# Scan stage: expanding an operand one chunk later on GpSimd, and loading it ahead of the values on SyncE

## The chip, the core and the metric

The kernel runs on one core of a Trainium2 chip. A core has TensorE (matmuls; PE in the profile, PEld for its weight loads), VectorE (DVE), ScalarE (ACT), GpSimd (POOL) and SyncE (SP), which issues the transfers between the device memory and the on-chip memory here. Each engine runs its own list of instructions in order; they wait for each other by semaphores. The metric is the device time of one execution in microseconds (us), as a median of several runs.

## The reference

A transformer block with adaptive layer norms: a linear-attention layer with a recurrent state, then two local-attention and feed-forward layers. Only the recurrence matters for this change. For each of 2 batches and 16 heads, with a state `s` of 16 x 16 and 4096 time steps:

```
def step(s, inp):
    q_, w_, k_, v_, a_, b_ = inp
    sa = einsum('bhij,bhj->bhi', s, a_)
    s = s * w_[:, :, None, :] + sa[..., None] * b_[:, :, None, :] + v_[..., None] * k_[:, :, None, :]
    return (s, einsum('bhij,bhj->bhi', s, q_))
```

The inputs of the step (q, w, k, v, a, b) are made by projections of a mixed `x` in the stage before; the output y goes through a group norm and a gate in the stage behind.

## The kernel before

The kernel has stages one after the other: setup, mix (the projections), scan (the recurrence), gate, and local (the two layers). The change is in the scan stage alone (`scan_stage`, lines 876 to 1489).

**Chunks and units.** The 4096 steps are cut into 256 chunks of 16 steps. Four chunks are a unit (`UC` = 4), and there are 64 units (`NU`), named by a pair: window `w` and half `k` (0 or 1). `shift(w, k, units)` names a unit further on. The state is carried from chunk to chunk, so the chunks of all heads run one after the other; within a chunk the work is matrix products of 32 x 32 blocks.

**The work of one chunk n.** TensorE (`chunk`, lines 1190 to 1219) runs ten groups of 32 small matmuls each. In order, by the tile they write: `P` from the state and `ax` (the second half of P; its first half, from `vc` and `d_ak`, was done at the end of the chunk before), `Y` from the state and `qx`, `Y` from `vc` and `d_qk`, `SA`, `S` from `vc` and `kT`; then `products` (lines 1160 to 1171) for a chunk 16 ahead, n + 16 (`LEAD` = 4 units ahead), which writes `AB` from `aq` and the expanded operands `bx` and `kx`; then `S` from `sa` and `bT`, and `Y` from `sa` and `d_qb`, whose end is signalled as `y_ps`; last the first half of P of chunk n + 1. The product AB of a chunk has to be known so early because it is masked, sent through device memory, inverted on VectorE (`solve`) and read back before the chunk itself runs. `products(n + 16)` stands in the loop only for the first 240 chunks.

**GpSimd** runs two kinds of work. `use(n)` expands the operands `ax`, `qx`, `bT` and `kT` of chunk n (six instructions) into buffers that exist twice, so it first waits for `y_ps` of chunk n - 2 (line 1124). `prepare(m)` expands `bx` and `kx` of chunk m (two instructions) from the tile `early` and signals `bk_x`, for which `products(m)` on TensorE waits (line 1162); it first waits for the transfer of `early` (line 1114) and for the product of chunk m - 2. ScalarE copies the third operand of the product, `aq`, from the same tile (`copy_aq`), at the end of each chunk, 17 chunks ahead.

**ScalarE** also copies the small results out of the matmul banks (`p`, `sa`, `y`) and the values `v` of the next chunk into `vc` (`copy_v`), for which the first half of P waits. **VectorE** keeps the state, masks AB, expands `d_ak` and `d_t`, and solves.

**SyncE** issues all transfers of the stage in one hand-written order (`unit`, lines 1060 to 1085). In each unit (w, k) it loads what the next unit needs (`part`, `tt`, `gl`), a problem for `solve`, on odd units (k = 1) four stores of y here and on even ones at the end, then in two halves (j = 0 and 1, two chunks each) `load_v` for the next unit, `load_early` for the unit five ahead and, after the first half, `load_late` (`late` and `tok`, for the unit two ahead), and at the end it stores a solution and the masked product (`pose`). `load_early(j)` waits until the product that reads the tile now is done (line 964); `load_v(j)` until ScalarE has copied the values that the tile holds now.

Of the kernel before, what the change touches and what calls it, by code (L numbers as in the profile page):

```python
# [875 lines left out]
def scan_stage(nc, persist, a, T):  # L876

    NU = 2 * (T // P)
    UC = NCH // 2
    BG = NB * CC  # L880
    LEAD = 4
    const, ident = persist["const"], persist["ident"]
    with ExitStack() as ctx:
# [44 lines left out]
        def shift(w, k, units):  # L928
            return w + (k + units) // 2, (k + units) % 2

        def first_chunk(w, k):
            return w * NCH + k * UC

        def bg(t):
            return t.rearrange("p b g i -> p (b g) i")
# [12 lines left out]
        def exists(w, k, units):  # L948
            return not isinstance(w, int) or 2 * w + k + units < NU

        with nc.Block() as block:
            @block.sync
            def _(sp):
# [8 lines left out]
                def load_early(w, k, j):  # L962

                    sp.wait_ge(S["ab_ps"].sem, S["ab_ps"].after(first_chunk(w, k) + 2 * j + 1, UC))
                    sp.sem_inc(s_free, 1)
                    sp.dma_start(early[j][:].rearrange("p c x b g y t -> p (c x b g y t)"),
                                 a["cm"][bass.ds(w, 1), :, k * UC + 2 * j:k * UC + 2 * j + 2].rearrange("o p c x b g y t -> (o p) (c x b g y t)")
                                 ).then_inc(pair["early_in"][j].sem, 16)
# [18 lines left out]
                def load_gl(w, k):  # L987
                    freed("s_sb", first_chunk(w, k) - 1 - UC)
                    sp.dma_start(gl[k][:].rearrange("p c q -> p (c q)"),
                                 a["gl"][bass.ds(w, 1), :, k * UC:(k + 1) * UC].rearrange("o p c b g -> (o p) (c b g)")  # L990
                                 ).then_inc(Hf["gl_in"][k].sem, 16)

                def load_part(w, k):

                    sp.wait_ge(Hf["part_out"][k].sem, Hf["part_out"][k].after(w))
                    for name in ("d_ak", "d_qk", "d_qb"):
                        freed(name, first_chunk(w, k) - 1 - UC)
                    sp.dma_start(part[k][:].rearrange("p c q z t -> p (c q z t)"),
                                 a["part"][bass.ds(w * 2 + k, 1)].rearrange("o p n -> (o p) n")).then_inc(Hf["part_in"][k].sem, 16)
# [10 lines left out]
                def load_problem(w, k):  # L1010
                    sp.wait_ge(Hf["att_out"][k].sem, Hf["att_out"][k].after(w))
                    sp.wait_ge(Hf["solved"][k].sem, Hf["solved"][k].after(w, 1))
                    sp.dma_start(prob[k][:, 0:SQ], a["att"][bass.ds(w * 2 + k, 1)].rearrange("o q h m t -> (o q h) (m t)")
                                 ).then_inc(Hf["prob_in"][k].sem, 16)

                def store_solution(w, k):
                    sp.wait_ge(Hf["solved"][k].sem, Hf["solved"][k].after(w))
                    sp.dma_start(a["inv"][bass.ds(w * 2 + k, 1)].rearrange("o q h m t -> (o q h) (m t)"), sol[k][:, 0:SQ]
                                 ).then_inc(Hf["inv_out"][k].sem, 16)

                def load_t(w, k):
                    sp.wait_ge(Hf["inv_out"][k].sem, Hf["inv_out"][k].after(w))
                    freed("d_t", first_chunk(w, k) - 1 - UC)
                    sp.dma_start(tt[k][:], a["inv"][bass.ds(w * 2 + k, 1)].rearrange("o (c q) h m t -> (o h m) c q t", c=UC)
                                 ).then_inc(Hf["tt_in"][k].sem, 16)

                def store_y(w, heads):
                    sp.wait_ge(Hf["yn"][1].sem, Hf["yn"][1].after(w))
                    for h in heads:
                        sp.dma_start(a["y_tok"][bass.ds(w, 1), :, :, :, :, h].rearrange("o t c b g i -> (o t) (c b g) i"),  # L1030
                                     yn[h * CH:(h + 1) * CH].rearrange("t c q i -> t (c q) i")).then_inc(y_out.sem, 16)
# [28 lines left out]
                def unit(w, k):  # L1060
                    heads = (range(HP // 2, HP) if k else range(HP // 2)) if not isinstance(w, int) or w > 0 else range(0)
                    if exists(w, k, 1):
                        n1 = shift(w, k, 1)
                        load_part(*n1)
                        load_t(*n1)
                        load_gl(*n1)
                    if exists(w, k, 3):
                        load_problem(*shift(w, k, 3))
                    if k and len(heads):
                        store_y(w - 1, heads)  # L1070
                    for j in range(UC // 2):
                        if exists(w, k, 1):
                            load_v(*shift(w, k, 1), j)
                        if exists(w, k, LEAD + 1):
                            load_early(*shift(w, k, LEAD + 1), j)
                        if j == 0 and exists(w, k, 2):
                            load_late(*shift(w, k, 2))
                    if exists(w, k, 2):
                        store_solution(*shift(w, k, 2))
                    if exists(w, k, LEAD):  # L1080
                        pose(*shift(w, k, LEAD))
                    if not k and len(heads):
                        store_y(w - 1, heads)
                    if not exists(w, k, LEAD):
                        fetch_weights(NU - 2 * w - k - 1)
# [19 lines left out]
            @block.gpsimd  # L1105
            def _(pool):
                def expand(dst, src):
                    return nc.gpsimd.tensor_tensor(dst[:], src.unsqueeze(2).broadcast_to([P, BG, HQ, CH]),  # L1108
                                                   headmask[:].unsqueeze(1).unsqueeze(3).broadcast_to([P, BG, HQ, CH]), ALU.mult)

                def prepare(w, k, c):

                    m = first_chunk(w, k) + c
                    pool.wait_ge(pair["early_in"][c // 2].sem, pair["early_in"][c // 2].after(w * 2 + k))
                    pool.wait_ge(S["ab_ps"].sem, S["ab_ps"].after(m, 2))
                    expand(bx[c % 2], bg(early[c // 2][:, c % 2, 1, :, :, 0, :]))
                    expand(kx[c % 2], bg(early[c // 2][:, c % 2, 1, :, :, 1, :])).then_inc(S["bk_x"].sem, 1)

                def use(w, k, c):

                    n = first_chunk(w, k) + c
                    if c == 0:
                        pool.wait_ge(Hf["late_in"][k].sem, Hf["late_in"][k].after(w))
                    pool.wait_ge(S["y_ps"].sem, S["y_ps"].after(n, 2))
                    expand(ax[c % 2], bg(late[k][:, c, :, :, 0, :]))
                    expand(qx[c % 2], bg(late[k][:, c, :, :, 1, :])).then_inc(S["ax_x"].sem, 1)
                    for dst, x in ((bT, 0), (kT, 1)):
                        for b in range(NB):
                            last = nc.gpsimd.tensor_tensor(  # L1129
                                dst[c % 2][:, b * CC:(b + 1) * CC], tok[k][:, c, b, x].unsqueeze(2).broadcast_to([P, CC, HQ, HS]),  # L1130
                                headmask[:].unsqueeze(1).unsqueeze(3).broadcast_to([P, CC, HQ, HS]), ALU.mult)
                    last.then_inc(S["kT_x"].sem, 1)

                pool.wait_ge(s_c, 48)
                for u in range(LEAD):
                    for c in range(UC):
                        prepare(u // 2, u % 2, c)
                prepare(LEAD // 2, 0, 0)
                use(0, 0, 0)
                use(0, 0, 1)  # L1140

                def unit(w, k):
                    for c in range(UC):
                        if c < UC - 1 and exists(w, k, LEAD):
                            prepare(*shift(w, k, LEAD), c + 1)
                        if c == UC - 1 and exists(w, k, LEAD + 1):
                            prepare(*shift(w, k, LEAD + 1), 0)
                        if c + 2 < UC:
                            use(w, k, c + 2)
                        elif exists(w, k, 1):  # L1150
                            use(*shift(w, k, 1), c + 2 - UC)

                halfwise(pool, unit)

            @block.tensor
# [1557 lines left out]
```

## Time and profile before

| | before |
|---|---|
| time, median of 3 runs | 5328.73 us (5325.01 to 5329.86) |
| profiled execution, its own time | 5325.01 us |
| its span (first to last instruction) | 5323.2 us |
| TensorE busy | 4869.5 us, 91% |
| VectorE busy | 3583.0 us, 67% |
| ScalarE busy | 3186.1 us, 60% |
| GpSimd busy | 2317.0 us, 44% |
| mean granted TensorE clock | 0.952 of full |

The profile also cuts the span into 40 slices of 133 us. The scan stage runs from slice 8 to slice 17 (about 960 to 2145 us): there TensorE is at 8 or 9 tenths, VectorE at 7, ScalarE at 4 or 5, GpSimd at 6 or 7, and the 16 DMA engines move 142 to 166 GB/s at a busy share of 6 or 7 tenths. So in this stage no engine is full, and the waits of each engine for the others have to be read. The local stage behind it (from about 2370 us) is most of the span, with TensorE over 9 tenths.

A busy share of TensorE counts overlapping matmuls once; its ends are modelled. "Idle before, releaser" in a row says how long the engine stood before the instruction and what ended that; "issue" means that the profile shows nothing that it waited for.

### The profile page before, as it was taken

The page shows a single profiled execution, that of the slowest core. Times are in us where ns is not written, and L with a number is a line of the kernel's source. Part 1 is how long each engine was busy: PE and PEld are TensorE (multiplying, and loading weights), DVE is VectorE, ACT ScalarE, POOL GpSimd, SP SyncE. Part 2 cuts the span into 40 slices and gives each one's busy share as a digit, 9 for nine tenths or more (in the row PEclk, how much of TensorE's full clock was granted, in tenths as well). Part 3 has the DMA queues.
Part 4 walks back from the last instruction along what each step waited for, and adds up shares of the span by engine and source line. Part 5 has one row for each costly group of instructions (what it writes and reads, how often), then busy time and mean ns, then how long its engine had stood idle before and what let it go on. Part 6 is the DMA issues. An engine that isn't in the chain of part 4 may idle for free. (4 is left out here: it accounts for less than half of the span.)

```text
span 5323.2 us, 277799 instructions
## 1 busy us (share of the span) xinstructions
PE 4869.5 (91%) x111000; PEld 4118.3 (77%) x111000; DVE 3583.0 (67%) x11241; ACT 3186.1 (60%) x8874; POOL 2317.0 (44%) x3833
## 2 busy tenths in 40 slices
PE   7988888588888888659999999999999999999999
PEld 6888888578888887547777777777777777777777
DVE  5666666577777776556666666666666666666665
ACT  5777777344444444346666666666666666666665
POOL 1222222466666666004444444444444444444443
PEclk8999999699999998779999999999999999999999
DMA  2433343677777777760000000000100000000000
GB/s 81 99 90 93 94 99 86 142 165 156 166 163 166 157 166 161 221 203 14 15 15 12 15 15 15 15 15 16 46 23 21 21 21 17 21 21 21 19 20 18
DMA packets 993729, 389.81 MB, mean 73 GB/s; under 512 B 773840, under 2 KB 938448, under 8 KB 992464
## 3 DMA queue, kind: packets, MB, share of 16 engines
q1 hardware_dynamic: 992256, 385.96, 30.7%
q14 instruction: 188, 1.54, 0.1%
q10 hardware_dynamic: 1232, 1.45, 0.1%
q8 instruction: 53, 0.87, 0.1%
HBM read 217.51 MB, written 169.74 MB: 73 GB/s over the span
## 5 line engine op out<-in xcount | busy, mean ns | idle before, releaser
L2303 ACT ACTIVATE l_prob<-l_prob,l_nb,l_rq 128x256 f32<-128x256 f32 x1024 | 604.6, 592 | 279.8 <-DVE l_nb L2089 278.2
L1954 POOL TENSOR_TENSOR l_pn<-l_prob,l_rinv 128x512 f32<-128x512 f32 x512 | 532.5, 1040 | 331.0 <-DVE l_rinv L2069 327.4
L2499 PE MATMUL lD<-l_hid,w 128*128 128x128 f32 x3072 | 384.8, 275 | 0.0
L2499 PEld LDWEIGHTS lD<-l_hid,w 128*128 128x128 f32 x3072 | 363.1, 192 | 0.2 <-issue 0.2
L2287 ACT COPY l_qT<-lA 128x512 f32<-128x512 f32 x128 | 74.9, 585 | 389.5 <-PE lA L2407 389.5
L1961 POOL TENSOR_TENSOR l_x1s<-l_x 128x128 f32<-128x128 f32 x128 | 58.0, 453 | 493.5 <-DVE l_x L2127 493.2
L497 POOL TENSOR_TENSOR rk<-rk,bkraw 128x256 f32<-128x256 f32 x64 | 54.6, 872 | 477.7 <-DVE bkraw L383 477.7
L2491 PE MATMUL lA<-l_hn,w 128*128 128x128 f32 x2048 | 258.2, 279 | 2.0 <-POOL l_hn L1972 2.0
L2465 PE MATMUL lB<-l_oT,wo 128*128 128x128 f32 x2048 | 259.9, 275 | 0.0
L2398 PE MATMUL lA<-wqkv,l_h 128*128 128x512 f32 x512 | 243.6, 598 | 16.4 <-DVE l_mask L2170 16.4
L2491 PE MATMUL lB<-l_hn,w 128*128 128x128 f32 x2048 | 249.6, 275 | 0.0
L2491 PEld LDWEIGHTS lA<-l_hn,w 128*128 128x128 f32 x2048 | 239.8, 192 | 9.4 <-POOL l_hn L1972 2.5
L2465 PEld LDWEIGHTS lB<-l_oT,wo 128*128 128x128 f32 x2048 | 243.7, 192 | 0.0
L1979 POOL TENSOR_TENSOR l_outt<-l_t,l_xat 128x256 f32<-128x256 f32 x64 | 46.4, 724 | 452.7 <-DVE l_t L2163 452.7
L2398 PE MATMUL lB<-wqkv,l_h 128*128 128x512 f32 x512 | 242.2, 595 | 0.0
L2398 PE MATMUL lC<-wqkv,l_h 128*128 128x512 f32 x512 | 240.6, 592 | 0.0
L2491 PEld LDWEIGHTS lB<-l_hn,w 128*128 128x128 f32 x2048 | 238.8, 192 | 0.0
L1451 DVE TENSOR_TENSOR sc_ssum<-sc_S,sc_state 128x64 f32<-128x64 f32 x256 | 57.0, 223 | 243.6 <-PE sc_S L1177 243.2
L1129 POOL TENSOR_TENSOR sc_kT<-sc_tok,sc_headmask 128x64 f32<-128x64 f32 x512 | 217.1, 443 | 0.0
L1108 POOL TENSOR_TENSOR sc_ax<-sc_late,sc_headmask 128x128 f32<-128x128 f32 x256 | 104.1, 407 | 236.2 <-PE sc_Y L1177 233.6
L2491 PE MATMUL lC<-l_hn,w 128*128 128x128 f32 x1536 | 205.3, 283 | 0.0
L1966 POOL TENSOR_TENSOR l_dsqs<-l_dsq 128x128 f32<-128x128 f32 x128 | 58.8, 459 | 333.2 <-ACT l_dsq L2316 333.2
(298 smaller groups left out, 15753.2 us busy)
## 6 DMA issues: line engine op xcount, KB each, us to landing
scratch_cm<-cm SPq DMA_DIRECT2D x64, 512.0 KB, 4.5
sc_early<-scratch_cm SPq DMA_DIRECT2D x128, 256.0 KB, 3.8
scratch_part<-sc_att SPq DMA_DIRECT2D x64, 512.0 KB, 6.4
sc_part<-scratch_part SPq DMA_DIRECT2D x64, 512.0 KB, 5.0
scratch_tok<-vt SPq DMA_DIRECT2D x512, 48.0 KB, 1.8
l_h<-scratch_h SPq DMA_DIRECT2D x128, 129.0 KB, 2.6
scratch_gr<-gr SPq DMA_DIRECT2D x64, 256.0 KB, 2.0
sc_late<-scratch_cm SPq DMA_DIRECT2D x64, 256.0 KB, 4.3
```

The lines of the kernel that those rows point to most:

```text
L1108: return nc.gpsimd.tensor_tensor(dst[:], src.unsqueeze(2).broadcast_to([P, BG, HQ, CH]), headmask[:].unsqueeze(1).unsqueeze(3).broadcast_t ...
L1129: last = nc.gpsimd.tensor_tensor(dst[c % 2][:, b * CC:(b + 1) * CC], tok[k][:, c, b, x].unsqueeze(2).broadcast_to([P, CC, HQ, HS]), headma ...
L1451: nc.vector.tensor_tensor(s_sum[:], first16(S_ps), state[c % 2][:], ALU.add).then_inc(S["s_sum"].sem, 1)
L1954: tt(pn[s][:, pair], prob[s][:, pair], rinv[s][:, pair].unsqueeze(2).broadcast_to([P, 2, 2 * P]), ALU.mult).then_inc(Q["pn"][s].sem, 1)
L1961: tt(x1s[s][:], shifted(x1[s][w])[:, 0:P], shifted(x1[s][w])[:, P:2 * P], ALU.add).then_inc(S["x1_sum"][s].sem, 1)
L1966: tt(dsqs[s][:], dsq[s][:, 0], dsq[s][:, 1], ALU.add).then_inc(S["dsq_sum"][s].sem, 1)
L2287: nc.scalar.copy(qT[s][:].rearrange("p h t -> p (h t)"), bank[s][0][:]).then_inc(S["qT"][s].sem, 1)
L2303: last_ = nc.scalar.activation(prob[s][:, h], prob[s][:, h], ACT.Exp, scale=rq8[s][:, h:h + 1], bias=nb[s][:, h:h + 1], accum_out=sums[s][ ...
L2398: last_ = mm(bank[s][j][:], h[:, k * P:(k + 1) * P], wqkv[:, k, j * INNER:(j + 1) * INNER], start=(k == 0), stop=(k == CC - 1))
L2465: last_ = mm(bank[s][1][:, m * P:(m + 1) * P], wo[:, k, m * P:(m + 1) * P], oT[s][:, k], start=(k == 0), stop=(k == NHP - 1))
L2491: last_ = mm(bank[s][j][0:MW, at:at + P], w1[:, k, tile * MW:(tile + 1) * MW], hn[s][:, k], start=(k == 0), stop=(k == CC - 1))
L2499: last_ = mm(bank[s][3][:, c * P:(c + 1) * P], w2[:, m, c * P:(c + 1) * P], hid[s][:, m], start=(c == 0 and m == 0), stop=(c == CC - 1 and ...
```

## The change

Two edits, both in `scan_stage`. On SyncE, `load_early` moves ahead of `load_v` in each half of a unit. On GpSimd, the preamble no longer prepares a 17th chunk, and in the loop the iteration of chunk n calls `prepare(n + 16)` and then `use(n + 2)`, where it called `prepare(n + 17)` and then `use(n + 2)`. ScalarE's `copy_aq` stays 17 chunks ahead, and TensorE's order is not touched.

```diff
--- before.py
+++ after.py
@@ -1069,10 +1069,10 @@
                     if k and len(heads):
                         store_y(w - 1, heads)
                     for j in range(UC // 2):
+                        if exists(w, k, LEAD + 1):
+                            load_early(*shift(w, k, LEAD + 1), j)
                         if exists(w, k, 1):
                             load_v(*shift(w, k, 1), j)
-                        if exists(w, k, LEAD + 1):
-                            load_early(*shift(w, k, LEAD + 1), j)
                         if j == 0 and exists(w, k, 2):
                             load_late(*shift(w, k, 2))
                     if exists(w, k, 2):
@@ -1135,16 +1135,13 @@
                 for u in range(LEAD):
                     for c in range(UC):
                         prepare(u // 2, u % 2, c)
-                prepare(LEAD // 2, 0, 0)
                 use(0, 0, 0)
                 use(0, 0, 1)
 
                 def unit(w, k):
                     for c in range(UC):
-                        if c < UC - 1 and exists(w, k, LEAD):
-                            prepare(*shift(w, k, LEAD), c + 1)
-                        if c == UC - 1 and exists(w, k, LEAD + 1):
-                            prepare(*shift(w, k, LEAD + 1), 0)
+                        if exists(w, k, LEAD):
+                            prepare(*shift(w, k, LEAD), c)
                         if c + 2 < UC:
                             use(w, k, c + 2)
                         elif exists(w, k, 1):
```

GpSimd's list, from the place where the preamble has issued `use(0)`. The digit behind a name is the buffer: chunk parity for `ax`, `bx` and so on, the half of a unit for `early`. Before:

```order
L1108 TENSOR_TENSOR sc_ax1<-sc_late0,sc_headmask 128x128 [waits sc_y_ps0]
L1108 TENSOR_TENSOR sc_qx1<-sc_late0,sc_headmask 128x128
L1129 TENSOR_TENSOR sc_bT1<-sc_tok0,sc_headmask 128x64 x2
L1129 TENSOR_TENSOR sc_kT1<-sc_tok0,sc_headmask 128x64 x2
L1108 TENSOR_TENSOR sc_bx1<-sc_early0,sc_headmask 128x128 [waits sc_ab_ps0,sl_early_in0]
L1108 TENSOR_TENSOR sc_kx1<-sc_early0,sc_headmask 128x128
L1108 TENSOR_TENSOR sc_ax0<-sc_late0,sc_headmask 128x128 [waits sc_y_ps0]
L1108 TENSOR_TENSOR sc_qx0<-sc_late0,sc_headmask 128x128
L1129 TENSOR_TENSOR sc_bT0<-sc_tok0,sc_headmask 128x64 x2
L1129 TENSOR_TENSOR sc_kT0<-sc_tok0,sc_headmask 128x64 x2
L1108 TENSOR_TENSOR sc_bx0<-sc_early1,sc_headmask 128x128 [waits sc_ab_ps0,sl_early_in1]
L1108 TENSOR_TENSOR sc_kx0<-sc_early1,sc_headmask 128x128
```

and now, from the same `use(1)`:

```order
L1108 TENSOR_TENSOR sc_ax1<-sc_late0,sc_headmask 128x128 [waits sc_y_ps0]
L1108 TENSOR_TENSOR sc_qx1<-sc_late0,sc_headmask 128x128
L1129 TENSOR_TENSOR sc_bT1<-sc_tok0,sc_headmask 128x64 x2
L1129 TENSOR_TENSOR sc_kT1<-sc_tok0,sc_headmask 128x64 x2
L1108 TENSOR_TENSOR sc_bx0<-sc_early0,sc_headmask 128x128 [waits sc_ab_ps0,sl_early_in0]
L1108 TENSOR_TENSOR sc_kx0<-sc_early0,sc_headmask 128x128
L1108 TENSOR_TENSOR sc_ax0<-sc_late0,sc_headmask 128x128 [waits sc_y_ps0]
L1108 TENSOR_TENSOR sc_qx0<-sc_late0,sc_headmask 128x128
L1129 TENSOR_TENSOR sc_bT0<-sc_tok0,sc_headmask 128x64 x2
L1129 TENSOR_TENSOR sc_kT0<-sc_tok0,sc_headmask 128x64 x2
L1108 TENSOR_TENSOR sc_bx1<-sc_early0,sc_headmask 128x128 [waits sc_ab_ps0,sl_early_in0]
L1108 TENSOR_TENSOR sc_kx1<-sc_early0,sc_headmask 128x128
```

Between `use(1)` (buffers 1) and `use(2)` (buffers 0) stood the expansion for chunk 17 (`bx1`), with that of chunk 16 done ahead of `use(0)`; now the expansion for chunk 16 (`bx0`) stands there. From here on every `bx`, `kx` pair belongs to the chunk one lower than before.

SyncE's list in the middle of a unit, the loads for the values, the early and the late operands, to the store of a solution. Before:

```order
L973 DMA sc_v0<-scratch_tok 128x4x32 [waits sc_v_c0]
L966 DMA sc_early0<-scratch_cm 128x512 [waits sc_ab_ps0]
L980 DMA sc_late0<-scratch_cm 128x4x128 [waits sc_kT_x0]
L983 DMA sc_tok0<-scratch_tok 128x8x64
L973 DMA sc_v1<-scratch_tok 128x4x32 [waits sc_v_c0]
L966 DMA sc_early1<-scratch_cm 128x512 [waits sc_ab_ps0]
L1018 DMA scratch_inv<-sc_sol0 128x256 [waits mxb_k30]
```

and now:

```order
L966 DMA sc_early0<-scratch_cm 128x512 [waits sc_ab_ps0]
L973 DMA sc_v0<-scratch_tok 128x4x32 [waits sc_v_c0]
L980 DMA sc_late0<-scratch_cm 128x4x128 [waits sc_kT_x0]
L983 DMA sc_tok0<-scratch_tok 128x8x64
L966 DMA sc_early1<-scratch_cm 128x512 [waits sc_ab_ps0]
L973 DMA sc_v1<-scratch_tok 128x4x32 [waits sc_v_c0]
L1018 DMA scratch_inv<-sc_sol0 128x256 [waits mxb_k30]
```

`early0` and `v0` have changed places, and so have `early1` and `v1`; `v1` now stands behind the wait for the product that `early1` waits for, and in front of the stores.

## Rows read from the trace of the kernel before

**Rows 1.** Busy time by stretch: columns stretch, length, engines, clock, DMA share, GB/s

```profile
1020.00:2060.00 1040.00, 897.01 (x75225) 834.25 (x75227) 806.70 (x2401) 503.80 (x2285) 723.17 (x1878) 0.93 0.77 162
1510.00:1516.00 6.00, 5.39 (x361) 5.19 (x365) 1.74 (x8) 2.14 (x10) 3.95 (x13) 0.50 1.10 217
```

**Rows 2.** Waits, 1020 to 2060: who waited for whom, total us, times, longest

```profile
POOL sc_ax L1108 <- PE sc_Y L1177: 193.2, 172, 8.0
POOL sc_bx L1108 <- DMA sc_early<-scratch_cm: 124.3, 37, 5.2
ACT sc_vc L1265 <- DMA sc_v<-scratch_tok: 61.9, 28, 3.1
ACT sc_aq L1259 <- DMA sc_early<-scratch_cm: 44.9, 29, 2.6
PE sc_P L1177 <- ACT sc_vc L1265: 19.9, 19, 1.9
PE sc_SA L1177 <- ACT sc_p L1282: 18.5, 24, 1.8
```

**Rows 3.** GpSimd's instructions in a chunk, timeline: start us, us, engine, line

```profile
1558.45 0.40 POOL L1108 TENSOR_TENSOR sc_ax<-sc_late,sc_headmask 128x128 f32<-128x128 f32 x1 [1.02 <-PE sc_Y L1177]
...
1559.90 1.38 POOL L1129 TENSOR_TENSOR sc_kT<-sc_tok,sc_headmask 128x64 f32<-128x64 f32 x2
1561.25 0.40 POOL L1108 TENSOR_TENSOR sc_bx<-sc_early,sc_headmask 128x128 f32<-128x128 f32 x1
1561.61 0.40 POOL L1108 TENSOR_TENSOR sc_kx<-sc_early,sc_headmask 128x128 f32<-128x128 f32 x1
```

**Rows 4.** TensorE, the same chunk

```profile
1557.86 0.48 PE L1177 MATMUL sc_Y<-sc_sa,sc_d_qb 32*32 32x32 f32 x32
1560.60 0.42 PE L1169 MATMUL sc_AB<-sc_aq,sc_bx 32*32 32x32 f32 x29 [0.15 <-issue]
1561.47 0.48 PE L1177 MATMUL sc_Y<-sc_sa,sc_d_qb 32*32 32x32 f32 x32
```

**Rows 5.** GpSimd and TensorE in the preamble: a wait on the expanded operand

```profile
986.01 0.43 POOL L1108 TENSOR_TENSOR sc_kx<-sc_early,sc_headmask 128x128 f32<-128x128 f32 x1
986.69 0.55 PE L1169 MATMUL sc_AB<-sc_aq,sc_bx 32*32 32x32 f32 x25 [2.67 <-POOL sc_kx L1108]
```

**Rows 6.** The chunk that waits for transfers, timeline, SyncE, ScalarE, GpSimd, TensorE

```profile
1509.25 0.45 PE L1177 MATMUL sc_P<-sc_vc,sc_d_ak 32*32 32x32 f32 x32 [1.07 <-ACT sc_vc L1265]
...
1542.12 0.40 SPq L973 DMA_DIRECT2D sc_v<-scratch_tok  x1
1542.88 0.33 SPq L966 DMA_DIRECT2D sc_early<-scratch_cm  x1
1544.51 0.24 ACT L1265 COPY sc_vc<-sc_v 128x64 f32<-128x64 f32 x1 [2.42 <-DMA sc_v<-scratch_tok]
1546.53 0.30 ACT L1259 COPY sc_aq<-sc_early 128x128 f32<-128x128 f32 x1 [1.20 <-DMA sc_early<-scratch_cm]
1546.59 0.40 POOL L1108 TENSOR_TENSOR sc_bx<-sc_early,sc_headmask 128x128 f32<-128x128 f32 x1 [3.90 <-DMA sc_early<-scratch_cm]
1547.30 0.40 POOL L1108 TENSOR_TENSOR sc_ax<-sc_late,sc_headmask 128x128 f32<-128x128 f32 x1
1549.38 0.40 POOL L1108 TENSOR_TENSOR sc_kx<-sc_early,sc_headmask 128x128 f32<-128x128 f32 x1
1544.90 0.45 PE L1177 MATMUL sc_P<-sc_vc,sc_d_ak 32*32 32x32 f32 x32 [1.30 <-ACT sc_vc L1265]
1548.29 0.65 PE L1169 MATMUL sc_AB<-sc_aq,sc_bx 32*32 32x32 f32 x32
1549.56 0.66 PE L1177 MATMUL sc_Y<-sc_sa,sc_d_qb 32*32 32x32 f32 x32
```

**Rows 7.** SyncE's queue, the unit before the next such place

```profile
1559.13 0.37 SPq L973 DMA_DIRECT2D sc_v<-scratch_tok  x1
1561.59 0.35 SPq L966 DMA_DIRECT2D sc_early<-scratch_cm  x1
```

## The prediction

> **What bounds the kernel now.** I read the waits of the scan stage first, then the busy time of one long stretch, then the timeline of single chunks on GpSimd, TensorE and SyncE.
>
> The stretch from 1020 to 2060 us holds 235 chunks (GpSimd's 1878 instructions there over 8 per chunk), so a chunk takes 1040.0 / 235 = 4.43 us [rows 1]. No engine is full in it: TensorE 897 us, VectorE 807, GpSimd 723. In the waits the reader sees two things [rows 2]. GpSimd stands idle before `ax` 172 times, 193.2 us, for the `Y` matmuls of TensorE: once per chunk it goes through its list, and then waits for the next `y_ps`. And there are waits for transfers: GpSimd before `bx` for `early` (37 times, 124.3 us), ScalarE for `v` (28 times, 61.9 us) and for `early` (29 times, 44.9 us). About 29 times is once in two units, that is once in eight chunks. Little of it reaches TensorE: 19.9 us behind the copied `v`, 18.5 us behind `p`.
>
> What that one chunk costs shows in rows 6: `v` is issued at 1542.12, copied at 1544.51 after 2.42 us of waiting, and TensorE starts at 1544.90, 1.30 us late. The stretch from the last end of `Y` to this one (1543.6 to 1550.2) is 6.6 us long. In the same place of the period before, 35 us earlier, TensorE waits 1.07 us for `vc` until 1509.25 [rows 6]; from 1510 the granted clock is 0.50 for 6 us, the level of 1.2 GHz, while TensorE is busy 5.39 of them [rows 1]. Such a chunk costs some 2.2 us more than the mean one. GpSimd's 3.9 us of waiting for `early` are not on the path: its `ax` (1547.30) is for a later chunk.
>
> The order around `products` decides the rest. In a chunk without stalls `Y` ends at 1557.86 + 0.48 = 1558.34, the matmuls of AB start at 1560.60, and the next `Y` ends at 1561.95 [rows 4]: 2.26 us, then 1.35 us. GpSimd starts `ax` at 1558.45, 0.11 us behind the first `Y`, and ends `kx` at 1562.01 [rows 3], 1.41 us after AB has started. That is harmless today, because this `kx` belongs to the chunk after.
>
> **The change on GpSimd.** The instructions are the same but for one pair in the preamble; the numbers of the pairs move. `use(n + 1)` waits for `y_ps(n - 1)` and now `prepare(n + 16)` stands behind it, where `prepare(n + 17)` stood. TensorE needs `bk_x(n + 16)` in the middle of chunk n. So a ring closes within one chunk: the end of `Y` of n - 1, six instructions of `use`, two of `prepare`, AB, `S`, `Y` of n. Before, a whole chunk lay between `kx` and its matmuls. The ring in four terms:
> - end of `Y` to `ax`: 0.11 us [rows 3, 4].
> - GpSimd's eight instructions: 723.17 us over 235 chunks, 3.08 us [rows 1]. Bounds: the shortest pass, the one behind the stall, is 1547.30 to 1549.78, 2.48 us [rows 6]; the pass in rows 3, with a pair of `kT` at 1.38 us, is 3.56. I take the mean, since the trigger (`y_ps`) and the list are unchanged and VectorE's work behind the same `y_ps` is too.
> - end of `kx` to AB: `kx` ends at 986.44 and AB starts at 986.69, 0.25 us [rows 5].
> - AB to the end of `Y`: 1.35 us [rows 4]; at the low clock 1548.29 to 1550.22, 1.93 us [rows 6]. The mean granted clock of 0.93 [rows 1] means the low level in 14% of the time, so 0.14 x 0.58 = 0.08 more.
>
> The ring is 0.11 + 3.08 + 0.25 + 1.35 + 0.08 = 4.87 us, against 4.43 for a mean chunk now, stalls included: +0.44. TensorE will stand before AB in nearly every chunk. With the two bounds for GpSimd it is 4.27 and 5.35 us, so -0.16 and +0.92 per chunk.
>
> A word on why GpSimd's pass differs so. A pair of `kT` takes 1.38 us where VectorE runs a product of two tiles beside it. The Trainium skill (SBUF — State Buffer, "SBUF: two separate sides") has a reason: GpSimd and a VectorE instruction with two inputs in that memory take turns on one pair of ports, for the whole instruction. By that rule the stretches stay, since VectorE's products stand behind the same signal; the sum would be the one above.
>
> The dropped pair in the preamble takes 2 x 0.4 us off GpSimd once; nothing to speak of.
>
> **The change on SyncE.** `early` goes out one issue sooner, 0.76 us by the distance of the two issues [rows 6]. This ends ScalarE's wait before `aq`. But `v`, the transfer on which TensorE waited, goes out later: by the 0.76 us; by as much again because `v` of the second half is now behind the wait for the product (before at 1559.13, ahead of `early` at 1561.59 [rows 7]; now after it, and all that follows, up to the next unit's `v`, moves down by that issue); and it lands behind `early`, which is larger and took 1542.88 to 1546.5, so up to 1.2 us more than the 2.4 of today [rows 6]. Together 1.5 to 2.7 us later. Against it, TensorE comes to the place later too: three rings of +0.44 are 1.3 us. So its wait at the first half of P, 1.3 us today, comes to 1.5 to 2.7. Up to 3.44 - 2.26 = 1.2 us of it lie beside GpSimd's part of the ring (0.11 + 3.08 + 0.25, against TensorE's own 2.26). What is left is 0.3 to 1.5 us in eight chunks; I take 0.6, or 0.08 per chunk. The 124.3 us of waiting before `bx` go to nearly nothing and give nothing: GpSimd only waits for `y_ps` instead.
>
> **Sum.** 4.87 + 0.08 = 4.95 us, against 4.43: +0.52 in each of the 240 chunks that have a product ahead, +125 us. The profiled execution took 5325.0 us (span 5323.2 and 1.8 around it), so 5450. It was the fastest of the three runs; against the median, 3.7 us above it, it is 5454 us, 2.3% slower.
>
> **Rivals.**
> *The value transfer becomes the bound.* If SyncE's list is what limits (its place before `v` is reached at 1542.12 after a run of issues without a pause), the later `v` is paid in full: 2.7 us more per eight chunks, and only the rings between are slower. 4.87 + 0.26 = 5.13, +0.70 x 240 = +168 us, 5497. For it: 28 waits for `v` already today. Against it: a longer period leaves SyncE more time between its waits for TensorE.
>
> *The clock falls more often.* TensorE will stand up to 1.4 us in a chunk, and today a low clock follows a stand of 1.07 us [rows 1, 6]. At the low clock a chunk's own path is 1544.90 to 1550.22, 5.3 us, waits in it included, so about 5.3 to 5.6. Half the time at it gives some 5.24 us on average, +0.81 x 240 = +195, 5524. Against it: today's stand comes once in eight chunks with the rest of its chunk stretched to 6.6 us, while the new ones leave a chunk at 4.95. The Trainium skill (TensorE: Matmul & The Clock Gate, "HAM oscillation — how this bites in real kernels") speaks for this rival: a loop in which TensorE keeps waiting falls back to the lower clock again and again. The trace agrees as far as the one place per eight chunks shows it.
>
> *Faster.* The ring does not bind: GpSimd's pass is near its shortest, 2.48 us, in most chunks, and the stall for the transfers is gone. Then 4.27 - 0.08 (clock) = 4.19 us, -0.24 x 240 = -58, 5271. It decides where the pass is below 4.43 - 1.35 - 0.11 - 0.25 - 0.08 = 2.64 us on average. For it: passes that start late, behind VectorE's products, are that short. Against it: only the late ones are, and the change makes none late.
>
> *Small.* The stalled chunk loses its 2.2 us whole (0.28 per chunk) and a pass takes 2.9: 0.11 + 2.9 + 0.25 + 1.35 = 4.61 against 4.43, +43 us, 5372.
>
> **How the numbers follow.** Forecast 0.67, own range 5415 to 5485. The value transfer 0.11, the clock 0.09, small 0.08, faster 0.05. The range of 8 in 10 reaches from 5395, near the small case, to 5515, past the value transfer and short of the clock case. A measurement of this kernel tells a change of about 0.2% (11 us) from none. Slower by more than that: the first four cases but for a tail of the small one, 0.92; faster 0.05; within it 0.03.
>
> **What would show it.** In the waits of the stage, TensorE before AB for GpSimd's `kx` should have over 180 entries and 100 us or more; GpSimd before `bx` for `early` should be nearly gone, and so ScalarE's wait before `aq`. The period should be near 4.95 us, `kx` ending just before AB starts, and GpSimd's busy time per chunk still 3.0 to 3.15 us. ScalarE's wait for `v` should remain. Wrong if the ring is not what TensorE waits for, if GpSimd's pass changes by more than 0.2 us, or if the clock in the stage falls below 0.85. The stages before and behind should keep their length.

## The result and the profile after

The changed kernel takes 5475.28 us (median of 4 runs, 5473.95 to 5481.69), against 5329.30 us for the kernel before (4 runs). The ratio is 1.0276, with a 95% interval of 1.0260 to 1.0294: 146 us or 2.8% slower. The forecast was 5454 us, with a range of 5395 to 5515.

| | before | after |
|---|---|---|
| profiled execution / its span | 5325.01 / 5323.2 us | 5473.54 / 5471.7 us |
| TensorE busy from 0 to 958 us (setup, mix) | 821.11 us | 821.02 us |
| first load of the gate stage | 2162.2 us | 2311.0 us |
| first matmul of the local stage | 2370.8 us | 2517.8 us |
| a chunk (stretch in the stage) | 4.43 us | 5.04 us |
| mean granted clock in that stretch | 0.93 | 0.88 |

The stages around the scan kept their length: the gate stage starts 148.8 us later and the local stage 147.0, and the whole span is 148.5 us longer. All of the loss lies in the scan.

The stretch of the stage, by the busy times of the engines (columns as in [rows 1]), holds 1856 / 8 = 232 chunks:

```profile
1020.00:2190.00 1170.00, 911.28 (x74269) 854.45 (x74269) 816.52 (x2371) 499.58 (x2259) 728.20 (x1856) 0.88 0.66 143
```

1170.0 / 232 = 5.04 us a chunk, and 728.20 / 232 = 3.14 us of GpSimd. The waits of the same stretch, against [rows 2] (who waited for whom, total us, times, longest):

```profile
POOL sc_ax L1108 <- PE sc_Y L1174: 445.3, 232, 9.4
...
PE sc_AB L1166 <- POOL sc_kx L1108: 202.0, 198, 1.8
ACT sc_p L1279 <- PE sc_P L1174: 162.5, 231, 1.2
ACT sc_vc L1262 <- DMA sc_v<-scratch_tok: 63.8, 25, 3.5
...
PE sc_P L1174 <- ACT sc_vc L1262: 4.7, 13, 1.0
```

The largest wait of TensorE is now the one before AB for GpSimd's `kx`, in 198 of 232 chunks, 202 us. In the kernel before it was next to nothing (1020 to 2060 us):

```profile
PE sc_AB L1169 <- POOL sc_kx L1108: 1.7, 10, 0.2
```

The two waits for `early`, 124.3 and 44.9 us before, are gone. GpSimd stands idle for 38% of the stretch (1170 - 728 us; before 30%, 1040 - 723), nearly all of it in the wait for `Y`, and still it is what TensorE waits for: the two engines take turns.

One turn in the timeline (start us, length us, engine, line), TensorE and GpSimd, against [rows 3, 4]:

```profile
1553.82 0.48 PE L1174 MATMUL sc_Y<-sc_sa,sc_d_qb 32*32 32x32 f32 x32
...
1554.42 0.40 POOL L1108 TENSOR_TENSOR sc_ax<-sc_late,sc_headmask 128x128 f32<-128x128 f32 x1 [1.69 <-PE sc_Y L1174]
...
1555.87 1.38 POOL L1129 TENSOR_TENSOR sc_kT<-sc_tok,sc_headmask 128x64 f32<-128x64 f32 x2
...
1557.57 0.40 POOL L1108 TENSOR_TENSOR sc_kx<-sc_early,sc_headmask 128x128 f32<-128x128 f32 x1
...
1558.20 0.42 PE L1166 MATMUL sc_AB<-sc_aq,sc_bx 32*32 32x32 f32 x29 [1.79 <-POOL sc_kx L1108]
...
1559.07 0.47 PE L1174 MATMUL sc_Y<-sc_sa,sc_d_qb 32*32 32x32 f32 x32
```

`Y` ends at 1554.30, `ax` starts 0.12 us later, `kx` ends at 1557.97, AB starts 0.23 us behind it, `Y` ends 1.34 us later: 5.24 us, and each step is released by the one before.

The chunk that was 6.6 us long before [rows 6] is one of 4.6 us now:

```profile
1619.18 0.24 ACT L1262 COPY sc_vc<-sc_v 128x64 f32<-128x64 f32 x1 [2.43 <-DMA sc_v<-scratch_tok]
...
1619.52 0.40 POOL L1108 TENSOR_TENSOR sc_ax<-sc_late,sc_headmask 128x128 f32<-128x128 f32 x1 [1.69 <-PE sc_Y L1174]
...
1619.57 0.45 PE L1174 MATMUL sc_P<-sc_vc,sc_d_ak 32*32 32x32 f32 x32 [0.16 <-ACT sc_vc L1262]
...
1622.07 0.40 POOL L1108 TENSOR_TENSOR sc_kx<-sc_early,sc_headmask 128x128 f32<-128x128 f32 x1
...
1622.70 0.42 PE L1166 MATMUL sc_AB<-sc_aq,sc_bx 32*32 32x32 f32 x29 [0.48 <-POOL sc_kx L1108]
```

ScalarE waits 2.43 us for `v` as before, but TensorE only 0.16 us for it. GpSimd's pass (its eight instructions from `ax` to `kx`) is 1619.52 to 1622.47 here, 2.95 us, where the one that started late took 2.48.

### The profile page after: what moved, and what is told of

The parts are those of the page before. It is cut to its first block and busy times, and to the rows that moved or that the text cites. A ratio compares the mean times of both kernels' runs of the same rounds, so it can differ in the third digit from the quotient of the medians.

```text
span 5471.7 us, 277771 instructions
## 1 busy us (share of the span) xinstructions
PE 4895.1 (89%) x111000; PEld 4150.3 (76%) x111000; DVE 3601.0 (66%) x11241; ACT 3189.2 (58%) x8874; POOL 2332.4 (43%) x3833
## 5 line engine op out<-in xcount | busy, mean ns | idle before, releaser
L1166 PE MATMUL sc_AB<-sc_aq,sc_bx 32*32 32x32 f32 x8192 | 127.9, 203 | 248.2 <-POOL sc_kx L1108 235.7
L1166 PEld LDWEIGHTS sc_AB<-sc_aq,sc_bx 32*32 32x32 f32 x8192 | 105.5, 116 | 270.6 <-issue 266.3
L1297 ACT COPY sc_y<-sc_Y 128x64 f32<-128x64 f32 x256 | 54.0, 211 | 388.9 <-PE sc_Y L1174 388.8
L1129 POOL TENSOR_TENSOR sc_kT<-sc_tok,sc_headmask 128x64 f32<-128x64 f32 x512 | 240.3, 488 | 0.0
```

The lines of the kernel that those rows point to most:

```text
L1129: last = nc.gpsimd.tensor_tensor(dst[c % 2][:, b * CC:(b + 1) * CC], tok[k][:, c, b, x].unsqueeze(2).broadcast_to([P, CC, HQ, HS]), headma ...
L1166: last = mm(AB_ps[c][at, (2 * q + x) * QH:(2 * q + x + 1) * QH], src[c][at, q].rearrange("p h t -> p (h t)"), aq[c][at, q], start=True, st ...
```

## The experiments

Theory: a ring, that is a chain of waits that closes on itself (end of `Y`, `use`, `prepare`, AB, `Y`), sets the period of the changed kernel. Rival: the transfers that SyncE now issues in another order do. Nine kernels were run. All ratios are to the kernel before, run on the same chip.

| kernel | us, median | ratio, 95% |
|---|---|---|
| GpSimd's edit alone | 5474.43 | 1.0276 (1.0259 to 1.0293) |
| SyncE's edit alone | 5374.30 | 1.0085 (1.0069 to 1.0102) |
| changed, `prepare` inside `use` | 5378.12 | 1.0095 (1.0079 to 1.0112) |
| changed, one more expansion | 5580.45 | 1.0471 (1.0454 to 1.0489) |
| before, one more expansion | 5329.64 | 1.0002 (0.9992 to 1.0012) |
| before, `v` ahead | 5328.70 | 1.0003 (0.9993 to 1.0012) |
| before, `v` and `early` ahead | 5276.02 | 0.9900 (0.9883 to 0.9916) |
| `v` and `early` ahead, GpSimd's edit, `prepare` inside `use` | 5277.46 | 0.9910 (0.9894 to 0.9927) |
| `v` and `early` ahead, GpSimd's edit | 5471.45 | 1.0274 (1.0257 to 1.0291) |

**GpSimd's edit alone.** The second hunk of the change, with the first left out:

```diff
-                prepare(LEAD // 2, 0, 0)
...
-                            prepare(*shift(w, k, LEAD), c + 1)
...
+                            prepare(*shift(w, k, LEAD), c)
```

> GpSimd's edit alone, SyncE's order as before. Theory (ring): the end of Y, six instructions of use, two of prepare, AB and the next Y close a ring within one chunk, so the whole loss is here: 5455 to 5485 us, TensorE before AB for GpSimd's kx some 200 us in about 200 waits. Rival (transfers): the loss of the changed kernel comes from v going out behind early; then this kernel is near the one before, 5330 to 5370 us, and that wait is short.

It has the whole loss, 5474.43 us against 5475.28 of both edits. The wait, 1020 to 2060 us:

```profile
PE sc_AB L1166 <- POOL sc_kx L1108: 190.2, 186, 1.9
```

ScalarE waits for `v` only 2.1 us in all here, and the loss is the same. The ring holds; the rival falls.

**SyncE's edit alone.** The first hunk only.

> SyncE's edit alone, GpSimd's list as before. Theory (ring): no ring, but v lands 1.5 to 2.7 us later with no longer period to cover it, less 0.4 us that ScalarE's wait before aq cost TensorE: 30 x (1.0 to 2.3) us = +30 to +70, so 5360 to 5400 us, and more than 28 waits or more than 61.9 us for v. Rival (transfers): most of the loss is here, 5430 to 5480 us.

Within the expected: 46 us slower than the kernel before. Waits of 1020 to 2060, one place in the timeline (SyncE, ScalarE, TensorE):

```profile
ACT sc_vc L1265 <- DMA sc_v<-scratch_tok: 125.7, 28, 5.3
...
PE sc_P L1177 <- ACT sc_vc L1265: 95.0, 27, 4.2
```

```profile
1524.70 0.34 SPq L966 DMA_DIRECT2D sc_early<-scratch_cm  x1
...
1525.38 0.39 SPq L973 DMA_DIRECT2D sc_v<-scratch_tok  x1
...
1529.58 0.24 ACT L1265 COPY sc_vc<-sc_v 128x64 f32<-128x64 f32 x1 [5.18 <-DMA sc_v<-scratch_tok]
...
1529.97 0.65 PE L1177 MATMUL sc_P<-sc_vc,sc_d_ak 32*32 32x32 f32 x32 [4.06 <-ACT sc_vc L1265]
```

ScalarE waits in 28 places as before, but TensorE for 3.5 us in each of 27, not for 1.0 in 19. `v` takes 4.2 us from its issue to its copy, where it took 2.4 [rows 6]: in this place the larger `early`, issued first, lands at 1529.13, and `v` at 1529.56. So this half of the change costs 46 us by itself and nothing beside the ring, whose longer chunks cover it.

**The changed kernel, `prepare` inside `use`.**

```diff
                     expand(qx[c % 2], bg(late[k][:, c, :, :, 1, :])).then_inc(S["ax_x"].sem, 1)
+                    if between:
+                        prepare(*between)
                     for dst, x in ((bT, 0), (kT, 1)):
```

`between` names the chunk for `prepare`; the loop passes it on to `use` and makes no call of `prepare` of its own.

> The changed kernel (both edits), but prepare(n + 16) stands inside use(n + 1), behind ax and qx and ahead of bT and kT. Theory (ring): the pass from Y to kx is 0.12 + 0.72 + 0.76 + 0.25 = 1.85 us, under TensorE's own 2.26, so the wait for kx goes (under 20 us) and the time falls to that of SyncE's edit alone or a little under: 5340 to 5400 us. Rival (transfers): the time stays at 5440 to 5480.

The instructions and the wait for `Y` ahead of them are the same; only four of the six that stood in the ring stand behind `kx` now. It gives back 97 of 146 us and lands on SyncE's edit alone (5378 and 5374). The wait that was 202 us, and the one that is left:

```profile
PE sc_P L1176 <- ACT sc_vc L1264: 86.3, 27, 3.7
...
PE sc_AB L1168 <- POOL sc_kx L1108: 13.0, 25, 0.7
```

**One more expansion, in the changed kernel and in the one before.** Each has this line more, and a pair of tiles that nobody reads:

```diff
                     expand(bx[c % 2], bg(early[c // 2][:, c % 2, 1, :, :, 0, :]))
+                    expand(spare[c % 2], bg(early[c // 2][:, c % 2, 1, :, :, 0, :]))
```

> The changed kernel with one more expansion in each prepare, of bx's data into a spare tile that nobody reads (0.36 us from start to start). Theory (ring): it is paid in full in 240 chunks, +0.36 x 240 = +86 us, so about 5560 us (5545 to 5580). Rival (transfers): GpSimd idles about 1.9 us a chunk before ax (445 us in 232 chunks), which would hide it: 5475 to 5490 us.

> The kernel before with the same additional expansion in each prepare as in the last kernel. Theory (ring): no ring here, GpSimd's pass of 3.08 + 0.36 = 3.44 us fits the chunk of 4.43, so 5325 to 5350 us (0 to +0.4%). Rival (GpSimd's own load is what counts wherever it stands): +86 us, 5415.

In the changed kernel it costs 105 us, in the kernel before 2 us, within its interval of nothing. The stretch 1020 to 2060 of each, first changed, then before:

```profile
1020.00:2060.00 1040.00, 787.37 (x60553) 745.87 (x60556) 668.52 (x1933) 410.81 (x1842) 660.38 (x1701) 0.80 0.60 131
```

```profile
1020.00:2060.00 1040.00, 894.27 (x75026) 831.12 (x75029) 818.28 (x2392) 502.52 (x2281) 803.54 (x2104) 0.94 0.77 162
```

The second has GpSimd busy for 803.54 us of 1040, more than the changed kernel has it (728.20 of 1170), and is not slower. So it is not GpSimd's load but its place in the ring. The 105 us are 19 more than a start-to-start of 0.36 us in 240 chunks (86), and put the time just above the range that was written for it. The rest goes with the granted clock, which fell from 0.88 to 0.80: over all chunks of the two stretches, the mean from the start of AB to the end of `Y` is 1.47 us in the changed kernel and 1.61 with the additional expansion, against 1.34 where the clock is high.

**`v` ahead, in the kernel before.** Two waits of the long chunk stood side by side, for `v` and for `early`. This takes one away:

```diff
                         n1 = shift(w, k, 1)
+                        load_v(*n1, 0)
                         load_part(*n1)
...
-                        if exists(w, k, 1):
+                        if j and exists(w, k, 1):
                             load_v(*shift(w, k, 1), j)
```

> The kernel before, with v of the first half loaded at the start of a unit on SyncE, ahead of part, tt and gl; nothing else moved. Theory A (two waits side by side): TensorE's wait for vc goes, but early lands when it did, ScalarE then waits 2.5 us or more before aq, p comes late by as much, and the time stays: 5315 to 5335 us. Theory B (v alone makes the long chunk): 30 x 1.3 to 2.2 us less, 5265 to 5290 us.

As theory A has it, the time stays: 5328.70 against 5327.76. Waits, and the place in the timeline:

```profile
ACT sc_aq L1260 <- DMA sc_early<-scratch_cm: 86.7, 28, 3.7
...
PE sc_SA L1178 <- ACT sc_p L1283: 58.3, 28, 2.6
```

```profile
1548.68 0.30 ACT L1260 COPY sc_aq<-sc_early 128x128 f32<-128x128 f32 x1 [3.35 <-DMA sc_early<-scratch_cm]
...
1548.88 0.21 ACT L1283 COPY sc_p<-sc_P 128x64 f32<-128x64 f32 x1
...
1549.35 0.42 PE L1178 MATMUL sc_SA<-sc_p,sc_d_t 32*32 32x32 f32 x29 [2.32 <-ACT sc_p L1283]
```

TensorE gets its `vc` at once and then stands 2.32 us before `SA`: ScalarE, in whose list `aq` is ahead of `p`, is held by `early`. The 18.5 us of this wait before became 58.3, the 19.9 us for `vc` none.

**`v` and `early` ahead, in the kernel before.** As the last, and `load_early` of the first half ahead of the stores of y:

```diff
+                    if exists(w, k, LEAD + 1):
+                        load_early(*shift(w, k, LEAD + 1), 0)
                     if k and len(heads):
                         store_y(w - 1, heads)
...
-                        if exists(w, k, LEAD + 1):
+                        if j and exists(w, k, LEAD + 1):
                             load_early(*shift(w, k, LEAD + 1), j)
```

> As the last one, and early of the first half is loaded ahead of the stores of y too, so both transfers land before TensorE comes to the place. The long chunk of 6.6 us becomes one of about 4.4: 30 x 1.5 to 2.2 us less, 5260 to 5285 us (1.0 to 1.3% faster), TensorE's wait for vc and ScalarE's before aq near nothing, the clock in the stage above 0.96. Rival (SyncE's list or the DMA engines are the limit of the period, 0.77 busy already): the waits move to another load or to the stores of y, and the time stays within 15 us of 5329.

52 us faster than the kernel before, 1.0%: this beats both kernels of the case. The last AB starts at 2023 us here, so the stretch is taken to 2000 us; the waits are those of 1020 to 2060:

```profile
1020.00:2000.00 980.00, 862.08 (x74418) 799.13 (x74409) 815.44 (x2380) 502.30 (x2262) 712.28 (x1858) 0.98 0.81 170
```

```profile
POOL sc_bx L1111 <- DMA sc_early<-scratch_cm: 81.3, 67, 3.3
...
DVE sc_yn L1441 <- DMA scratch_y_tok<-sc_yn: 32.4, 28, 2.1
...
ACT sc_aq L1262 <- DMA sc_early<-scratch_cm: 15.7, 20, 1.4
...
PE sc_SA L1180 <- ACT sc_p L1285: 2.6, 6, 0.7
```

A chunk takes 980 / (1858 / 8) = 4.22 us, not 4.43, which is 50 us in 240 chunks: the one chunk in eight that was 6.6 us long takes 4.2 on the mean. The clock is 0.98, not 0.93. TensorE's wait for `vc` is gone, and the one before `SA` is down to 2.6 us. Part of the rival is seen too: VectorE now waits in 28 places for the stores of y.

**GpSimd's edit on top of that, inside `use` and behind it.** Their diffs are the two already shown, on the kernel of 5276 us.

> The kernel with v and early loaded ahead (5276 us), and prepare(n + 16) inside use(n + 1), between qx and bT, on GpSimd. Theory: the ring of 1.85 us stays under TensorE's 2.26, so no wait for kx; GpSimd's waits for early there (81.3 us in 67) shrink and give nothing, since it then waits for Y: 5268 to 5285 us, the same as without it. Rival: the later preparation gives the transfers room that TensorE gets, 5250 to 5265 us.

> The kernel with v and early loaded ahead (5276 us), with GpSimd's edit of the changed kernel. Theory (the ring alone sets the period, whatever SyncE does): 5465 to 5480 us, like GpSimd's edit alone. Rival (part of the loss of the changed kernel is left from the transfers): 5276 + 146 = 5422 us or less.

The waits of GpSimd for `early` in the first, and of TensorE in the second:

```profile
POOL sc_bx L1111 <- DMA sc_early<-scratch_cm: 20.4, 28, 1.6
```

```profile
PE sc_AB L1169 <- POOL sc_kx L1111: 183.9, 184, 1.9
```

The first takes GpSimd's wait for `early` from 81.3 to 20.4 us and gains nothing (5277.46 us; ScalarE's wait before `aq` is 40.4 us there, 15.7 without). The second is at 5471.45, whatever SyncE does: behind the ring the better transfers, worth 52 us without it, leave no mark (ratios 1.0274 with them and 1.0276 without).

## Why the prediction was right, and where its sizes were off

**The ring is the bound.** It named the wait of TensorE before AB for `kx`, over 180 entries and over 100 us; there are 198 and 202.0 us. Taking four instructions out of the ring, or putting one in, moved the time as the theory said, and putting one into GpSimd's list where there is no ring did not.

**The period was too small.** 4.95 us were forecast, 5.04 measured: +0.62 for +0.52, and 0.62 x 240 = 148 us. By the terms, each as the mean over all chunks of the stretch:
- end of `Y` to `ax`, 0.11 forecast: 0.12 in most chunks, 0.16 on the mean, since it is 0.3 to 0.57 in 26 chunks. Why, no run shows; I had taken the term from a single chunk.
- GpSimd's pass, 3.08: 3.14. I took the mean of a stretch in which one pass in eight ran late and undisturbed, in 2.48 us. In the changed kernel that pass starts on time, beside VectorE's work, and takes 2.95; 0.47 / 8 = 0.06 is the difference.
- `kx` to AB, 0.25: 0.24 in most chunks, 0.26 on the mean.
- AB to `Y`, 1.35 and 0.08 for the low clock, 1.43 together: 1.34 at the high clock, 1.47 on the mean. A clock of 0.88 is 24% of the time at the low level, 0.24 x 0.58 = 0.14 by the same working.
- the later `v`, 0.08: TensorE's wait for `vc` is 4.7 us in 232 chunks, 0.02 in each, and most of that lies beside GpSimd's pass.

The four terms of the ring make 0.16 + 3.14 + 0.26 + 1.47 = 5.03 us, where 4.87 was forecast: the ring was mis-sized by 0.16, all of it on the short side. The 0.08 that was added for `v` was hardly paid and covered half of that, so the forecast of 5454 us came nearer by luck than its terms deserve.

**The step on SyncE** was right in kind and its size in the changed kernel too high. ScalarE still waits 25 times for `v`, 63.8 us, but TensorE comes to the place so late itself that only 13 of these reach it, with 4.7 us: 0.16 us in eight chunks, where 0.6 was taken. By itself the edit costs 46 us, within what was written for it before it ran.

**The rivals.** The value transfer did not become the bound: SyncE's edit moves the changed kernel by 1 us. (That rival had a wrong price: 2.7 us in eight chunks is 0.34 a chunk, not 0.26, which gives 5.21 us and about 5516. The measured time is under both.)

The clock did fall more than in the sum, to 0.88, but not to the half time at the low level of that rival; its share is 0.04 to 0.06 us a chunk. With the waits of TensorE at their least the mean clock is 0.98, in the kernel before 0.93, in the changed one 0.88, and 0.80 with one expansion more. The rule of the Trainium skill (TensorE: Matmul & The Clock Gate, "HAM oscillation — how this bites in real kernels"), that a loop which keeps waiting falls back to the lower clock, pointed the right way.

The faster case needed a mean pass under 2.64 us; the shortest pass of GpSimd in the changed kernel takes 2.75. The small case needed 2.9, and it was 3.14.

The prediction also named the rule of the Trainium skill (SBUF — State Buffer, "SBUF: two separate sides") by which GpSimd and VectorE take turns on a pair of ports. The trace agrees in that the pass that lost its late start grew from 2.48 to 2.95 us; no run here separates the ports from another cause.

## What to carry to other kernels

A large wait of an engine off the path can be worth nothing when taken away (GpSimd's for `early`, from 81.3 to 20.4 us, gained nothing); what counts is how much later the work may be done before someone on the path asks for it. Before moving work to a later place in an engine's list, write down what the engine waits for just ahead of the new place, and follow that back: if it is released by the consumer's own last step, a ring is closed, and the period cannot be shorter than its length. With `prepare` inside `use` the ring is closed too, but at 1.85 + 1.35 = 3.2 us, an estimate from the rows, it is shorter than the chunk of 4.43, and TensorE's wait for it is 13.0 us in 1040. Where two transfers hold up one place, look whether both must come earlier: `v` alone only moved the wait to the next instruction in ScalarE's list. (`early` alone, with `v` left in its place, was not run.)

## What the runs showed that I had not expected

The granted clock followed small waits: a mean wait before AB of 202.0 / 232 = 0.9 us in a chunk of 5.04, none longer than 1.8 us, went with 0.88, while the kernel before, with its stand in one chunk of eight, had 0.93. The sum had left the clock as it was. That the waits alone lower the clock is argued from this order of the kernels; no run changed only them.

Two neighbouring edits of one change did not add up: 146 us and 46 us alone, 146 us together. A cost behind a ring is hidden by it, and comes back when the ring is mended (5378 us, not 5329).
